# Narrow attentions of a fused decoder: heads in float32 in four row tiles, instead of bfloat16 parts stacked through DRAM

## The reference

```python
scores = jnp.einsum('bhqd,bhkd->bhqk', q, k) / np.sqrt(HEAD_DIM)
attn = jax.nn.softmax(scores, axis=-1)
out = jnp.einsum('bhqk,bhkd->bhqd', attn, v)
```

## Time and profile before

| | |
|---|---|
| median of three runs | 2733.49 us |
| the profiled execution | 2742.32 us, its span 2740.4 us |
| TensorE matmul busy | 2209.5 us (81%) |
| VectorE busy | 1557.6 us (57%) |
| ScalarE busy | 1388.0 us (51%) |
| GpSimd busy | 431.3 us (16%) |
| granted TensorE clock, mean | 0.89 |
| row maxima of the narrow stages (L1217) | 384 x 686 ns |
| exponentials of the narrow stages (L1303) | 384 x 596 ns |
| TensorE idle until a stack had come from DRAM | 93.3 us, 21 times |

### The profile page before, as it was taken

How to read it: one execution, slowest core, us unless ns; L and a number is a source line. 1 busy time by engine, 2 the same in 40 slices (tenths; PEclk the granted TensorE clock), 3 DMA queues, 4 the chain that set the end, 5 groups by cost and what they waited for, 6 DMA issues and landing times. The chain is left out here.

```text
span 2740.4 us, 42755 instructions
## 1 busy us (share of the span) xinstructions
PE 2209.5 (81%) x15323; PEld 1503.6 (55%) x15323; DVE 1557.6 (57%) x3627; ACT 1388.0 (51%) x2801; POOL 431.3 (16%) x462
## 2 busy tenths in 40 slices
PE   6899738879999998377715789999989466887999
PEld 4666624457777776133503456665667352445777
DVE  6777757666556563565586356666545435843111
ACT  4666326667767773255531466666521223662442
POOL 2111022033222221310143200010000012100000
PEclk9999959989899998599867899999989767988999
DMA  3000013200000000231100000000010103300000
GB/s 161 1 1 2 1 48 85 39 31 1 1 1 1 1 2 0 69 74 29 63 0 0 9 1 1 1 1 1 1 72 1 45 7 87 78 1 1 1 1 16
DMA packets 66464, 64.30 MB, mean 23 GB/s; under 512 B 7217, under 2 KB 60497, under 8 KB 65105
## 3 DMA queue, kind: packets, MB, share of 16 engines
q1 hardware_dynamic: 66257, 61.58, 8.1%
HBM read 51.05 MB, written 10.51 MB: 22 GB/s over the span
## 5 line engine op out<-in xcount | busy, mean ns | idle before, releaser
L463 PE MATMUL bank<-scratch 64*128 64x256 bf16 (+5 forms) x3656 | 395.7, 323 | 131.3 <-DMA scratch<-parts 93.3
L463 PEld LDWEIGHTS bank<-scratch 64*128 64x128 bf16 (+3 forms) x3656 | 220.7, 124 | 277.8 <-issue 83.1
L1217 DVE TENSOR_REDUCE scratch<-bank 128x2 f32<-128x512 f32 x384 | 246.0, 686 | 136.8 <-PE bank L463 133.8
L463 PE MATMUL bank<-w_keep,scratch 128*128 128x128 f32 (+4 forms) x1760 | 250.1, 337 | 34.4 <-ACT scratch L800 20.8
L463 PE MATMUL bank<-w_early,scratch 128*128 128x128 f32 (+3 forms) x2016 | 261.6, 316 | 10.9 <-ACT w_early L3091 8.5
L1303 ACT ACTIVATE w_keep<-bank 128x512 f32<-128x512 f32 x384 | 210.3, 596 | 106.8 <-PE bank L463 101.1
L463 PEld LDWEIGHTS bank<-w_early,scratch 128*128 128x128 f32 (+3 forms) x2016 | 220.8, 191 | 78.5 <-issue 53.6
L463 PE MATMUL bank<-XNT,w_early 128*128 128x512 f32 (+1 forms) x640 | 241.9, 516 | 5.4 <-ACT XNT L377 1.6
L463 PE MATMUL bank<-XNT,w_keep 128*128 128x256 f32 (+4 forms) x800 | 238.8, 438 | 8.3 <-POOL w_keep L2152 2.5
L463 PEld LDWEIGHTS bank<-w_keep,scratch 128*128 128x128 f32 (+3 forms) x1760 | 186.4, 188 | 95.8 <-issue 43.7
L3374 DVE SCALAR_TENSOR_TENSOR X<-bank,scratch,X 128x128 f32<-128x128 f32 x272 | 76.6, 345 | 221.1 <-PE bank L463 221.1
(11 more groups left out here) (407 smaller groups left out, 3788.0 us busy)
## 6 DMA issues: line engine op xcount, KB each, us to landing
scratch<-parts SPq DMA_DIRECT2D x768, 32.0 KB
parts<-scratch SPq DMA_DIRECT2D x24, 384.0 KB, 3.3
w_early<-pack_l3f SPq DMA_DIRECT2D x1, 4758.0 KB, 14.3
w_keep<-pack_l2f SPq DMA_DIRECT2D x1, 2124.0 KB, 12.4
w_early<-pack_mamba SPq DMA_DIRECT2D x1, 2120.0 KB, 19.1
w_keep<-pack_l2x SPq DMA_DIRECT2D x1, 2049.0 KB, 7.7
w_keep<-taps SPq DMA_DIRECT2D x4, 512.0 KB, 5.7
w_keep<-wave_kernels SPq DMA_DIRECT2D x1, 2048.0 KB
```

The source lines that it names most:

```text
L463: return pe.matmul(out, lhsT, rhs, start=start, stop=stop, skip_group_check=True)
L1217: dve.tensor_reduce(neg[:, :, h], self.k.bank[5 - g % 2][:, :].rearrange("p (t s) -> p t s", s=S), AXX, ALU.max, negate=True).then_inc(*s. ...
```

## The change

Queries and keys stay float32 and where they are. `spread_pool` (GpSimd) makes six masked copies of 128 x 256 for a batch: two of the queries, each with half of the heads' rows zeroed, and four of the keys, in each of which of every 32 partitions only the 8 of one head are left, and one more row, that of the head of the other query copy, is set to 1. A head is now addressed as the 32 rows in which it lies (`place`: row tile g modulo 4, query copy j // 2, key copy j): its score half is one float32 matmul of 32 rows, of which 8 carry the product. Heads follow each other through the four row tiles, so the two weighed and the two compared heads of a step lie in four different ones.

The row maxima are written straight into a padded tile at the column whose row is the 1 of the key copy. For each half of a batch's heads they are transposed in float32 and added to the query copy in place (`take_off_dve`), so the weigh matmul gives the scores less their maxima by itself. `SEL`, the three parts, the DRAM trip, `cut_maxima_dve` and the whole SyncE program of these stages go. Comparing runs 7 steps ahead instead of 10, the lead-in is 16 steps instead of 24 (`FIRST`), and the other jobs of the eight places are: project (b+2), value (b+1), maxima 1 (b), turn 0, turn 1, back (b-1), maxima 0 (b+1), out (b-1).

```diff
+    AHEAD = 7
+    FIRST = -16
...
+    def place(self, g):
+        return g // H, g % LANES, g % H // LANES
+    def query(self, g):
+        b, r, j = self.place(g)
+        return self.queries[b % 3].rearrange("p (n s) -> p n s", s=S)[32 * r:32 * (r + 1), j // 2, :]
+    def key(self, g):
+        b, r, j = self.place(g)
+        return self.keys[b % 3].rearrange("p (j s) -> p j s", s=S)[32 * r:32 * (r + 1), j, :]
...
     def weigh_and_compare_pe(self, pe, p):
...
-            for i in range(2):
-                g, rows = a + i, slice(HW * i, HW * (i + 1))
-                if g >= 4:
-                    pe.wait_ge(*s.weighed.at("e", g - 4))
-                mm(pe, k.bank[g % 4][:, :], k.SEL[rows, h + i, :], self.negt[b % 3][rows, :].unsqueeze(1).to_broadcast([HW, HALVES, S]), True, False)
-        if compares and x % H == 0:
-            pe.wait_ge(*s.loaded_stack(x // H % 3).at(x // H))
-        for i in range(2):
-            g, y = a + i, x + 1 - i
-            if compares and y - 2 >= 0:
-                pe.wait_ge(*s.maxed.at("x", y - 2))
-            for c in range(HALVES):
+        if weighs and p % 4 == 0:
+            pe.wait_ge(*s.formed.at(f"neg {p // 4 % 2}", a // H))
+        if compares and x % H == 0:
+            pe.wait_ge(*s.pool.at("spread", x // H))
+        for i in range(2):
+            if weighs and a + i >= 4:
+                pe.wait_ge(*s.weighed.at("e", a + i - 4))
+            if compares and x + i >= 2:
+                pe.wait_ge(*s.maxed.at("x", x + i - 2))
+        for c in range(HALVES):
             for i in range(2):
+                g, y = a + i, x + i
...
     def maximum_dve(self, dve, g):
...
-        dve.tensor_reduce(neg[:, :, h], self.k.bank[5 - g % 2][:, :].rearrange("p (t s) -> p t s", s=S), AXX, ALU.max,
+        dve.tensor_reduce(self.pad(b, half)[:, :, column], self.k.bank[4 + g % 2][:, :].rearrange("p (t s) -> p t s", s=S), AXX, ALU.max,
...
+    def take_off_dve(self, dve, kind, b):
+        s, half = self.k.s, int(kind[-1])
+        q = self.queries[b % 3][:, half * S:(half + 1) * S]
+        dve.wait_ge(*s.rolled.at(kind, b))
+        dve.tensor_tensor(q, q, self.k.bank[7][:, 0:S], ALU.add).then_inc(*s.formed.up(kind, b))
...
+    def spread_pool(self, pool, b):
...
+        for n in range(2):
+            pool.tensor_scalar(self.queries[b % 3][:, n * S:(n + 1) * S], q, masks[:, n:n + 1], None, ALU.mult)
+        for j in range(LANES):
+            o = pool.tensor_scalar(self.keys[b % 3][:, j * S:(j + 1) * S], key, masks[:, 2 + j:3 + j], masks[:, 6 + j:7 + j], ALU.mult, ALU.add)
```

More of the change, by code:

```diff
@@ L493, in score_pe @@
             pe.wait_ge(*s.weighed.at("e", g - 3))
[L494 to L495 removed]
         for t in range(HALVES):
[L497 removed]
+            m = mm(pe, bank[:, t * S:(t + 1) * S], q[:, t * P:(t + 1) * P], key)
         m.then_inc(*s.scored.up("s", g))
@@ L1086, in __init__, with pad @@
         self.vals = [tmp3(k, HALVES * H * VALUE_WIDTH) for _ in range(2)]
[L1088 to L1094, removed]
+    def place(self, g):
[6 more added lines that the diff above has]
+        return self.keys[b % 3].rearrange("p (j s) -> p j s", s=S)[32 * r:32 * (r + 1), j, :]
+    def pad(self, b, half):
+        return self.pads[b % 2][half].rearrange("p (t n) -> p t n", n=P)
     def lane_values(self, b):
@@ L1101, in other @@
         r, i = divmod(p, H // 2)
-        kind, b = (("project", r + 3), ("value", r + 1), ("turn 0", r - 1), ("turn 1", r - 1), (None, 0), ("back", r - 1), ("out", r - 1),
-                   ("neg", r + 1))[i]
-        there = kind is not None and 0 <= b < B
+        kind, b = (("project", r + 2), ("value", r + 1), ("neg 1", r), ("turn 0", r - 1), ("turn 1", r - 1), ("back", r - 1), ("neg 0", r + 1),
+                   ("out", r - 1))[i]
+        there = 0 <= b < B
         if there and self.projection is None and kind in ("project", "value"):
@@ L1198, in other_pe @@
         else:
-            pe.wait_ge(*s.cut.at("neg", b))
+            half = int(kind[-1])
+            pe.wait_ge(*s.maxed.at("x", b * H + 8 * half + 7))
             for t in range(HALVES):
-                m = pe.transpose(bank[:, :].bitcast(BF16)[:, t * P:(t + 1) * P], self.pads[b % 2].rearrange("p (t n) -> p t n", n=P)[:, t, :], k.IDB[:, :])
+                m = pe.transpose(bank[:, t * P:(t + 1) * P], self.pad(b, half)[:, t, :], k.w["ident"])
             m.then_inc(*s.rolled.up(kind, b))
@@ new lines, in maximum_dve @@
+        if g % 8 == 0:
+            if b >= 2:
+                dve.wait_ge(*s.rolled.at(f"neg {half}", b - 2))
+            else:
+                dve.wait_ge(*s.preset.at("pads"))
+        dve.tensor_reduce(self.pad(b, half)[:, :, column], self.k.bank[4 + g % 2][:, :].rearrange("p (t s) -> p t s", s=S), AXX, ALU.max,
+                          negate=True).then_inc(*s.maxed.up("x", g))
+    def take_off_dve(self, dve, kind, b):
[3 more added lines that the diff above has]
+        dve.tensor_tensor(q, q, self.k.bank[7][:, 0:S], ALU.add).then_inc(*s.formed.up(kind, b))
@@ L1242, in divide_dve @@
     def divide_dve(self, dve, kind, b):
         s, t = self.k.s, int(kind[-1])
-        sums = self.k.bank[7][:, :].rearrange("p (h w) -> p h w", w=VALUE_WIDTH)
+        sums = self.k.bank[7][:, :].rearrange("p (j r w) -> p j r w", r=LANES, w=VALUE_WIDTH)
         inv, out = self.inverse[b % 2][:, t * H:(t + 1) * H], self.O[b % 2][:, t * D:(t + 1) * D]
@@ L1274, in other_dve @@
             self.divide_dve(dve, kind, b)
+        elif kind in ("neg 0", "neg 1"):
+            self.take_off_dve(dve, kind, b)
         elif kind == "out":
@@ L1313, in act @@
                 if b >= 2:
-                    act.wait_ge(*s.pool.at("cut", b - 2, 3))
+                    act.wait_ge(*s.pool.at("spread", b - 2))
                 for n in range(2):
@@ L1334, in preset_pool @@
         for x in self.pads:
-            m = pool.memset(x, 0.0)
+            for half in x:
+                m = pool.memset(half, 0.0)
         m.then_inc(*s.preset.up("pads"))
@@ L1475, in pool @@
         for b in range(B):
[L1476 removed]
+            core.spread_pool(e, b)
             if b == 1:
@@ L3770, in pool @@
     def pool(e):
-        e.memset(k.ONE[:, :], 1.0).then_inc(*s.preset.up("one"))
         need(k, e, "l0", "consts")
@@ L3824, in build @@
         k.kern_dram = dram["wave_kernels"]
-        k.parts_dram = [nc.dram_tensor(f"parts_{n}", [P, 6 * S], BF16, kind="Internal").ap() for n in range(2)]
         walk(k, lambda name, program: program(Null()))
@@ L3933 @@
         arrays["pack_" + name] = pack
-    sel = np.zeros((P, H, P), mybir.dt.np(BF16))
-    for h in range(H):
-        for rows in (0, HW):
-            sel[rows + h:rows + 3 * H:H, h, :] = 1
-    arrays["sel"] = sel
     pairs = np.zeros((P, NWIDE * P + 32), np.float32)
```

148 lines of the change are left out of this document (30 added, 118 removed).

## The result

The changed kernel takes 2816.0 us (median of 4 runs, 2813.59 to 2817.54), the kernel before 2732.44 (4 runs, 2725.69 to 2744.07): a ratio of 1.030, with a 95% interval of 1.028 to 1.032. The forecast was 2800 (2740 to 2900). The profiled execution took 2813.59 us, its span 2811.8, against a span of 2740.4 before.

A forecast was written before the change was run, and what follows sets the result against it. The prediction took compares and row maxima, in series through the order of waits, as the bound: 84 us lost less 23 gained in the lead-ins is 61, so 2795 from the median, plus 5 for small waits: 2800 us (2740 to 2900).

The forecast's parts named there:

- The step in series: Narrow-stage steps: one wait for both maxima puts compare and two maxima in series, 84 us lost over three stages.
- The sign: What the profile after should show: TensorE idle ahead of most odd steps, 0.4 us or more in over 100 steps.
- Its size: A full step at full clock: 1.13 + 0.10 + 1.29 = 2.52 us, where it was 2.14.
- Four row tiles at once: A step's float32 score matmuls on TensorE run in four row tiles together: block done after 1.13 us.
- the rival of pairs: Only two of four row tiles run at a time: 0.85 us more on 171 steps, 2945 us; chance 0.07.
- The lead-in: First projected tensor to first exponential: 32.2 us against 39.5, 40.9 and 39.1, 22.9 us gained over three stages.
- The spread: GpSimd's masked copies in the lead-in, replacing the DRAM trip: 2 x 0.95 + 4 x 1.0 = 5.9 us.
- The clock in the steady part: Rival: TensorE's clock falls in a quarter of the narrow stages' steady steps, 71 us more, 2870; chance 0.13.
- the bound on TensorE: Rival: maxima and matmuls overlap, TensorE's own work of 17.1 us bounds a batch, 2690 us; chance 0.07.
- The 5 us for small waits: Added to the 2795 us sum, because the same kind of sum for before missed small waits: 14.3 of 17.1 us.
- The lower end of the forecast's own range: Range 2750 to 2840, allowing for a full clock in the lead-in and 0.06 us less a step; chance 0.69.
- The base: The 61 us sum was set on the profiled execution's 2742.3 us, 8.8 above the median, giving 2795 from the median.

The follow-up runs named there:

- experiment 1: Changed kernel with each row maximum taken over the first 128 of 256 keys, leaving out part of the computation: 2746.2 us, ratio 1.0035.
- experiment 2: Changed kernel with three compare banks instead of two and three weigh banks instead of four: 2743.8 us, ratio 1.0027.
- experiment 9: Changed kernel with three compare and three weigh banks, and the sums of four heads cut in halves, one half in each step: 2714.9 us, ratio 0.992.
- Experiment 4: Kernel before with the changed kernel's order, both waits ahead and second halves last, bfloat16 parts and DRAM kept: 2756.2 us, ratio 1.0082.
- experiment 3: Changed kernel comparing 8 steps ahead instead of 7, so weighed and compared heads share two row tiles: 3260.0 us, ratio 1.193.
- experiment 5: Changed kernel with three compare and three weigh banks, comparing 6 steps ahead instead of 7: 3028.4 us, ratio 1.103.
- experiment 8: Changed kernel with the two idle row tiles of compare-only steps filled by matmuls that nobody reads: 2814.7 us, ratio 1.0272.
- experiment 11: Changed kernel with three-and-three banks, halved sums, first copies signalled early, and unread matmuls filling all four row tiles in compare-only lead-in steps: 2691.9 us, ratio 0.984.

## Why the prediction was right

*The step in series* was the deciding step, and it held: score matmuls, two maxima, score matmuls, with TensorE idle until a maximum ends 117 times, 1.0 us each. The sign named the wrong steps: the idle time stands ahead of the even steps, not the odd ones, as the working itself has it (on odd steps there are no sums to lie beneath the maxima). Experiments 1 and 2 shorten the series in two independent ways, and leave 10 and 7 us of the 84 by which the change is slower. That is net of the lead-ins, which they shorten too. Behind the first exponentials the change lost 95.5 us; by the profiles experiment 1 gives back 58.5 of them, experiment 2 55.8 and experiment 9 82.6. Experiment 4 puts the series into the kernel before, where it costs 0.8%.

*Its size* was 2.52 and is 2.61. The block ends 0.05 us later than the two-tile row let expect, and the signals take 0.14, not 0.10; why they do was not tested. Over a batch that is 21.55 instead of 20.9, over 21 full batches 14 us; the loss behind the first exponential is 95.5, where I had 84, so this term more than covers the difference.

*Four row tiles at once*: 1.13 expected, 1.15 measured, 2.07 in two (experiment 3). The Trainium skill (TensorE: Matmul & The Clock Gate, on packing small matmuls) has a speedup of 3.07 for four row tiles; the factor here, four against two, is 1.8, and no run has one tile alone. The prediction made 1.1 us of that figure. From its own rows it comes to more: a pass is 0.265 us in the earlier trace rows (1.06 for four), sixteen are 4.24, and 4.24 / 3.07 is 1.38. The 1.13 that went into the sum came from the rows and not from there. In the same way the rival of pairs priced four more passes at 0.85 us, where the earlier trace rows give 1.06; experiment 3 has the block 0.92 longer and the step 0.83, so that price came near by luck.

*The lead-in* gained 27.1 us, not 22.9. The spread was mis-sized: 4.0 us (2 x 0.92 + 4 x 0.55) instead of 5.9. Doubling the columns from 128 did not double the time, and the operation with an addition was the shorter one. The compare-only step was 3.51 (381.57 to 385.08), 3.46 expected, at the clock of 0.50 that I took.

*The clock in the steady part* stayed at 1.00, so that rival fell, as did the pairs of tiles and the bound on TensorE. The 5 us for small waits that I added are shown by no run as a term of their own. The lower end of the forecast's own range, 2750, is below what its two terms give: 7.5 us a stage and 0.06 us on each of 171 steps are 33 us, which is 2767.

*The base.* The terms came to 66 us in the forecast; between the two profiled executions the difference is 71.3. The other 12 us of the medians' difference of 83.6 are where these executions lay: before's 10 us above its median, the one after 2.4 below. A sum made against one execution carries its scatter. That 2800 came within 16 us of 2816 is in part luck, as the lost time (11.5 us short) and the lead-in's gain (4.2 us short) were off in opposite directions.

## What to carry to other kernels

Before moving a wait, write down which buffers are in flight: with two banks and both waits ahead of the step, producer and consumer alternate, and each one's time counts in full. Count the series (block, one or two consumers, signals) against the engine's own work, and give each step some of the other work to lie beneath it; a third bank and halved sums brought 3.7% here (1.0298 to 0.992). Where row tiles are dealt out by an index, check that what runs side by side falls into different ones.

## What was not expected of the hardware

The granted clock was 0.50 with TensorE busy 24.15 of 25 us (experiment 3) and 24.91 of 25 (experiment 5), while the scores used two row tiles of 32; with four tiles and 13.31 of 17 us it was 1.00 (the changed kernel). It stayed at 0.50 with four tiles and 1.46 us idle in each step of 3.55 (experiment 8), and rose to 1.00 with four tiles and no idle time (experiment 11). So neither the time with a matmul nor the number of tiles sorts these rows alone; what does stays open. Filling idle tiles and idle time with matmuls that nobody reads paid 23 us here, 0.8% of the whole kernel.
